# Another order in linear attention, and the first expert sequence's gates and spreading inside its last steps

## What is computed

```python
def linear_attention(x, W_qkv, W_out):
    q, k, v = heads(x @ W_qkv.T)
    q = (elu(q) + 1) * D ** -0.5;  k = elu(k) + 1
    # the result doesn't depend on the size of the chunks
    attn = einsum('bhld,bhmd->bhlm', q, k) * causal
    num = attn @ v + q @ S         # S, Z: sums over the tokens before
    den = attn.sum(-1) + q @ Z
    return (num / maximum(den, 1e-6)) @ W_out.T

def experts(u, centroids, biases, Wr, br, Ws, bs):
    s = softmax(u @ centroids.T + biases)
    g = top-2 of s, zero elsewhere
    routed = einsum('bse,bseo->bso', g, einsum('bsd,eod->bseo', u, Wr) + br)
    return u + routed + (u @ (Ws[0] + Ws[1]).T + bs.sum(0)) / 2
```

## Time and profile before

| | us |
|---|---|
| median of 3 runs (lowest, highest) | 1292.22 (1291.72, 1292.61) |
| the profiled execution | 1292.3 |
| its span | 1290.4 |
| TensorE, VectorE, ScalarE, GpSimd busy | 1151.3, 980.8, 780.4, 563.2 |
| mean granted clock of TensorE | 0.968 |

### The profile page before, as it was taken

One profiled execution on the slowest core, in us unless ns is written; L12 is line 12 of the kernel. 1 busy time (PEld: TensorE's weight loads), 2 busy tenths in 40 slices (PEclk: granted clock), 3 DMA queues, 4 the chain that ended last, 5 costly groups with the idle time before them and its releaser, 6 DMA issues.

```text
span 1290.4 us, 32081 instructions
## 1 busy us (share of the span) xinstructions
PE 1151.3 (89%) x10554; PEld 949.4 (74%) x10554; DVE 980.8 (76%) x2499; ACT 780.4 (60%) x2324; POOL 563.2 (44%) x719
## 2 busy tenths in 40 slices
PE   3888885798989779999999999999999976999997
...
DMA packets 14303, 12.32 MB, mean 10 GB/s; under 512 B 1778, under 2 KB 12564, under 8 KB 13972
## 3 DMA queue, kind: packets, MB, share of 16 engines
...
...
## 4 chain that ended last, share of the span: by engine, by line
PE 45%; DVE 19%; issue 13%; POOL 4%; ACT 2%; DVEq 1%; POOLq 0%; ACTq 0%
PE bank L170 10%; PE bank L955 10%; PE bank L1049 9%; PE bank L1062 5%; PE bank L1020 5%; DVE work L1035 4%; PE bank L819 3%; POOL rstd L344 2%; DVE stat L277 2%; DVE work L1215 2%; DVE work L1207 2%; DVE yn L293 1%; PE bank L774 1%; POOL X L349 1%; DVE fh_hi L1176 1%
## 5 line engine op out<-in xcount | busy, mean ns | idle before, releaser
L972 ACT ACTIVATE work<-bank,work 128x256 f32<-128x256 f32 x512 | 236.0, 473 | 67.1 <-DVE work L964 66.5
L964 DVE TENSOR_REDUCE work<-bank 128x2 f32<-128x512 f32 x256 | 164.2, 684 | 119.6 <-PE bank L955 119.6
L986 POOL TENSOR_TENSOR work<-work 128x512 f32<-128x512 f32 x64 | 66.7, 1042 | 291.3 <-DVE work L980 291.3
L938 POOL TENSOR_TENSOR work<-work 128x512 f32<-128x512 f32 x128 | 164.2, 1283 | 30.8 <-DVE work L930 20.5
L992 ACT ACTIVATE work<-work 128x256 f32<-128x256 f32 x384 | 161.7, 510 | 0.0
L1020 PE MATMUL bank<-ident,work 128*128 128x128 f32 x1024 | 142.2, 281 | 4.9 <-POOL work L986 1.6
L1020 PEld LDWEIGHTS bank<-ident,work 128*128 128x128 f32 x1024 | 113.3, 143 | 36.9 <-issue 24.8
L819 PE MATMUL bank<-WrT,moe_work 128*128 128x128 f32 x1024 | 138.6, 279 | 0.7 <-POOL moe_work L796 0.7
L342 POOL TENSOR_SCALAR ve<-mv 128x2 f32<-128x2 f32 x128 | 28.8, 225 | 243.4 <-DVE mv L282 243.4
L955 PE MATMUL bank<-work 32*128 32x256 f32 x2048 | 131.0, 393 | 3.5 <-DVE work L930 1.7
L1049 PE MATMUL bank<-work 128*64 128x256 f32 x1024 | 127.2, 390 | 6.9 <-DVE work L1035 6.9
...
## 6 DMA issues: line engine op xcount, KB each, us to landing
...
```

Of the source, the lines that this page charges most:

```text
L938: nc.gpsimd.tensor_tensor((QT if kind == "q" else KT)[:, p, a, :], rc[:, ru % 2, :], rs_[:, ru % 2, :], ALU.add).then_inc(c_rope, 1)
L964: nc.vector.tensor_reduce(nmax[:, QUAD * a + j, :], SB_[j][:, :].rearrange("p (t k) -> p t k", t=T), AX.X, ALU.max, negate=True).then_inc( ...
L972: ins = nc.scalar.activation(pr[:, a % 2, j, t, :], SB_[j][:, t * LEN:(t + 1) * LEN], ACT.Exp, bias=nmax[:, h, t:t + 1], accum_out=psum_[: ...
```

## The change

The steps of the linear attention are reordered on three engines. On TensorE the v product comes right behind scores(i, 0), ahead of sums and of the transposition of xn, the output product behind that transposition; ktok, qk and the state product come between sums(i, 0) and their transposition back. v no longer waits for the copied xn; the transposition of o does. On VectorE neg is first in the step and feat is ahead of the statistics of y. On ScalarE the exp is first, the blocks come ahead of the second mask copy, ktok's copy ahead of the sums'. GpSimd makes xT of expert sequences 0 and 1 in steps 14 and 15, TensorE's router for sequence 0 runs inside step 15, and its gates, low half and first three spreadings and scaled products are placed among the remaining attention work. The normalisation of sequence 15 moves into expert steps 0 and 1, three of the ternary check's parts move to expert steps or ahead of them, the two Wsh operations move into attention steps 2 and 3, and the spreading uses its four banks in another order.

The diff, cut (left out: context, and on each engine hunks that only follow from those shown):

Shared functions and GpSimd:

```diff
     pool.wait_ge(last_use, reached(per_seq * (i - 1)))
-    if l == MOE and i_is(i, 0, 1):
-        pool.wait_ge(a_v, SEQS)
+    if l == MOE:
+        if i_is(i, 0, 1):
+            pool.wait_ge(a_v, SEQS - 1 + i)
         pool.wait_ge(n_xnT[1], i + 1)
...
     pe.wait_ge(a_state, reached(i - 1))
-    pe.wait_ge(n_xnT[1], reached(i - 3))
     for t in range(T):
...
 XPAIRS = EXPERTS // 2
-RB, XB, YB_M = bank[1], bank[2:6], bank[6:8]
+RB, XB, YB_M = bank[1], (bank[4], bank[5], bank[3], bank[2]), bank[6:8]
 DVE_PAIRS, FAR = 3 * XPAIRS // 4, 3
...
             pool.wait_ge(z_xnT, CHUNKS)
-        if not i_is(i, SEQS - 2, SEQS - 1):
+        if i_is(i, SEQS - 2, SEQS - 1):
+            pool_xT(pool, MOE, i - (SEQS - 2), p)
+        else:
             pool_xT(pool, LA, i + 2, p)
...
             norm_pool(pool, 1, i - LA_LAG, 1)
+        if not i_is(i, 0, 1, SEQS - 1):
             ffn_excess_pool(pool, i - LA_LAG, p)
...
-    pool_xT(pool, MOE, 0, 0)
-    pool_xT(pool, MOE, 1, 1)
-    for i in range(SEQS - LA_LAG, SEQS):
-        for k in range(ROUNDS[1]):
-            norm_pool(pool, 1, i, k)
-    for i in range(SEQS - LA_LAG, SEQS):
-        ffn_excess_pool(pool, i, i % 2)
-    pool.wait_ge(n_xnT[1], SEQS)
+    rstd_pool(pool, 1, SEQS - 2, 0)
+    residual_pool(pool, 1, SEQS - 2)
+    rstd_pool(pool, 1, SEQS - 2, 1)
+    ffn_excess_pool(pool, SEQS - 3, 1)
...
         if not i_is(i, SEQS - 1):
             moe_far_pool(pool, i + 1, FAR)
+        if i_is(i, 0, 1):
+            ffn_excess_pool(pool, SEQS - 2 + i, p)
```

VectorE:

```diff
         more, live = not i_is(i, SEQS - 1, SEQS), not i_is(i, SEQS)
+        if more:
+            la_feat_vector(dve, i + 1, 1 - p, 0)
         if not i_is(i, 0):
...
                 la_mask_vector(dve, i, 0, g)
+        if more:
+            la_feat_vector(dve, i + 1, 1 - p, 1)
         if not i_is(i, 0, 1):
             run_piece(1, n1, 0, i - LA_LAG, p)
-        if more:
-            la_feat_vector(dve, i + 1, 1 - p, 0)
         if not i_is(i, 0):
...
             run_piece(1, n1, 1, i - LA_LAG, p)
-        if more:
-            la_feat_vector(dve, i + 1, 1 - p, 1)
         if live:
...
         moe_router_vector(dve, rch, 0, 0, part)
-    la_step(SEQS, 0)
-    run_piece(1, n1, 3, SEQS - 2, 0)
+    la_state_vector(dve, SEQS - 1)
+    la_divide_vector(dve, SEQS - 1, 0)
+    run_piece(1, n1, 3, SEQS - 3, 1)
     for part in range(MOE_EXP_PART, MOE_ROUTER_PARTS):
...
     rch.end()
-    for k in range(len(n1)):
-        run_piece(1, n1, k, SEQS - 1, 1)
+    run_piece(1, n1, 0, SEQS - 2, 0)
+    la_divide_vector(dve, SEQS - 1, 1)
+    run_piece(1, n1, 1, SEQS - 2, 0)
     moe_low_vector(dve, 0, 0)
-    for k in range(FAR):
-        moe_scaled_vector(dve, 0, k)
+    moe_scaled_vector(dve, 0, 0)
+    moe_scaled_vector(dve, 0, 1)
+    run_piece(1, n1, 2, SEQS - 2, 0)
+    moe_scaled_vector(dve, 0, 2)
+    run_piece(1, n1, 3, SEQS - 2, 0)
     rch.begin(1)
...
+MOE_LAST_NORM = (1, 2, 5, 7)
 MOE_ORDER = (("norm", 0), ("norm", 1), ("pair", 4), ("late", 4), ("late", 5), ("late", 6), ("late", 7), ("pair", 5),
...
         for what, part in MOE_ORDER:
-            if what == "norm" and not i_is(i, 0):
-                run_piece(2, n2, part, i - 1, 1 - p)
+            if what == "norm":
+                if not i_is(i, 0):
+                    if i_is(i, 1) and part == len(n2) - 1:
+                        dve.wait_ge(n_tp[1], SEQS)
+                    run_piece(2, n2, part, i - 1, 1 - p)
+                elif part in MOE_LAST_NORM:
+                    run_piece(1, n1, MOE_LAST_NORM.index(part), SEQS - 1, 1)
             if what == "early" and not i_is(i, SEQS - 2, SEQS - 1):
```

ScalarE:

```diff
         more, live = not i_is(i, SEQS - 1, SEQS), not i_is(i, SEQS)
+        if more:
+            la_exp_scalar(act, i + 1)
         if live:
             la_mask_scalar(act, i, 0)
+        if more:
+            la_v_scalar(act, i + 1, 1 - p)
         if not i_is(i, 0):
...
         if more:
-            la_v_scalar(act, i + 1, 1 - p)
-            la_exp_scalar(act, i + 1)
+            la_blocks_scalar(act, i + 1, 1 - p)
         if live:
...
             la_turn_scalar(act, i - 1)
-        if more:
-            la_blocks_scalar(act, i + 1, 1 - p)
         if live:
-            la_sums_scalar(act, i, 0)
             la_ktok_scalar(act, i)
+            la_sums_scalar(act, i, 0)
         if not i_is(i, 0, 1, 2):
...
     moe_router_scalar(act, 0, 0)
-    la_step(SEQS, 0)
-    norm_scalar(act, 1, SEQS - 2, TB[:, 0:LEN])
+    la_sums_scalar(act, SEQS - 1, 1)
+    norm_scalar(act, 1, SEQS - 3, TB[:, 0:LEN])
     moe_gates_scalar(act, 0, 0)
-    norm_scalar(act, 1, SEQS - 1, TB[:, 0:LEN])
+    la_turn_scalar(act, SEQS - 1)
+    norm_scalar(act, 1, SEQS - 2, TB[:, 0:LEN])
     act.wait_ge(s_w[SA], 16 * 4)
```

TensorE:

```diff
             la_scores_tensor(pe, i, p, 0)
-        if not i_is(i, 0, 1):
-            la_out_tensor(pe, i - 2)
+        if more:
+            la_v_tensor(pe, i + 1, 1 - p)
         if not i_is(i, 0):
...
         if not i_is(i, 0, 1, 2):
+            pe.wait_ge(a_va, at_most_all(i + 2))
             pe.wait_ge(a_state, i)
             norm_tensor(pe, 1, i - LA_TURN_LAG, TB)
-        if more:
-            la_v_tensor(pe, i + 1, 1 - p)
+        if not i_is(i, 0, 1):
+            la_out_tensor(pe, i - 2)
         if not i_is(i, 0):
...
             la_scores_tensor(pe, i, p, 1)
-        if i_is(i, SEQS - 1, SEQS):
-            pe.wait_ge(n_xnT[1], i - LA_TURN_LAG + 1)
+        if i_is(i, SEQS - 1):
+            pe.wait_ge(s_w[MOE], 16 * 4)
+            pe.wait_ge(a_feat, SEQS)
+            moe_router_tensor(pe, 0, 0)
         if not i_is(i, 0):
+            pe.wait_ge(n_xnT[1], reached(i - LA_TURN_LAG + 1))
             la_turn_tensor(pe, i - 1)
...
             la_sums_tensor(pe, i, p, 0)
+            la_ktok_tensor(pe, i, p)
         if not i_is(i, SEQS - 2, SEQS - 1, SEQS):
...
         if live:
-            la_ktok_tensor(pe, i, p)
-            la_back_tensor(pe, i, 0)
             la_state_tensor(pe, i, p)
+            la_back_tensor(pe, i, 0)
     over_sequences(pe, la_step, 4)
...
-    pe.wait_ge(s_w[MOE], 16 * 4)
-    pe.wait_ge(a_feat, SEQS)
-    moe_router_tensor(pe, 0, 0)
-    la_step(SEQS, 0)
-    la_out_tensor(pe, SEQS - 1)
-    norm_tensor(pe, 1, SEQS - 2, TB)
+    la_sums_tensor(pe, SEQS - 1, 1, 1)
+    pe.wait_ge(a_state, SEQS)
+    norm_tensor(pe, 1, SEQS - 3, TB)
+    la_out_tensor(pe, SEQS - 2)
+    la_back_tensor(pe, SEQS - 1, 1)
     moe_gates_tensor(pe, 0, 0)
-    norm_tensor(pe, 1, SEQS - 1, TB)
-    pe.wait_ge(n_xnT[1], SEQS)
-    pe.wait_ge(a_m, (G4 - 1) * T * SEQS)
-    pe.wait_ge(a_me, T * SEQS)
-    pe.wait_ge(a_o, T * SEQS)
-    pe.wait_ge(n_yn[1], SEQS)
+    pe.wait_ge(n_xnT[1], SEQS - 2)
+    la_turn_tensor(pe, SEQS - 1)
     pe.wait_ge(s_wsh, 2)
...
     pe.wait_ge(s_brlo, 1)
-    for k in range(4):
+    for k in range(FAR):
         moe_spread_tensor(pe, 0, 0, k)
+    la_out_tensor(pe, SEQS - 1)
+    norm_tensor(pe, 1, SEQS - 2, TB)
+    pe.wait_ge(n_xnT[1], SEQS - 1)
+    moe_spread_tensor(pe, 0, 0, FAR)
     moe_router_tensor(pe, 1, 1)
...
                 moe_spread_tensor(pe, i + 1, 1 - p, k - 4)
+            if k == 0 and i_is(i, 1):
+                norm_tensor(pe, 1, SEQS - 1)
             if k == 0 and not i_is(i, 0, 1):
+                if i_is(i, 2):
+                    pe.wait_ge(n_xnT[1], SEQS)
                 norm_tensor(pe, 2, i - 2)
```

39 lines of the change are left out of this document (21 added, 18 removed).

## The result

| | us |
|---|---|
| median of 4 runs (lowest, highest) | 1281.88 (1278.90, 1283.82) |
| beside it the kernel before, 4 runs | 1291.97 |
| ratio, 95% interval | 0.9923 (0.9908 to 0.9938) |
| the profiled execution, its span | 1278.9, 1277.1 |

The change saves 10.1 us. I had forecast 24.6, and 1281.88 lies 3.9 us above the end of my range. The stretches of the profile after show which half came. Busy time of each engine by stretch; the columns are those of the earlier trace rows.

What follows compares the result with a forecast made beforehand. TensorE comes nearest to bounding steady attention steps; between the stages no engine is half busy. Terms -12.8 - 1.7 - 12.4 + 1.0 + 1.3 = -24.6 us gave 1267.5 us, range 1257 to 1278.

Steps and rivals of the forecast that it cites:

- The attention steps, -12.8: Linear attention steps 4 to 14: each falls from 11.07 to 9.91 us, saving 12.8 us (8.9 to 15.7).
- What is late next is VectorE: Steady attention step: VectorE's 9.31 us of busy time plus a 0.60 us wait for rstd give 9.91 us.
- my upper bound of 10.26: Steady attention step: VectorE's present occupation with its short gaps, 9.66 us, plus the rstd wait, at most 10.26 us.
- rival C: Attention steps don't shorten: VectorE, waiting for out, back and rstd, stays near 11 us; 1281 us, chance 0.07.
- My lower bound: Steady attention step: no shorter than the 9.64 us that TensorE alone needs.
- Rival B: Attention steps: VectorE and GpSimd obstruct each other, every xn slow, step 10.22 us; 1271 us (up to 1276), chance 0.18.
- Steps 0 to 3, -1.7: First attention steps, held by GpSimd: TensorE's 1.29 us wait in step 2 goes; 1.7 us saved (0 to 2.7).
- The stretch between the stages, -12.4: From scores(15, 0) to the first expert product: 28.8 us instead of 41.2, sums at the slow clock; 12.4 us saved.
- rival A: Between the stages the clock stays at its full level: -28.9 us in all, 1263.4 us, at best 1257; chance 0.14.
- Rival D: Between the stages no overlap: gates held, spreading still after sequence 15's rows, only steps shorten; 1279 us, chance 0.05.
- Given back, +2.3: First expert steps: +1.0 us for slow clock and sequence 15's normalisation, +1.3 for rstd behind GpSimd's check products.
- Rival E: Attention steps: GpSimd's rstd late behind mask and check products, making the kernel slower, 1302 us with 3 us lateness; chance 0.03.

Runs made afterwards that it cites:

- out_mid: Changed kernel with TensorE's output product moved between the second sums and the transposition of the norm; 1275.30 us, ratio 0.9870.
- after_again: The changed kernel unaltered, run and profiled a second time, against the kernel before; 1282.78 us, ratio 0.9924.

## Why the prediction was right and wrong

- **The attention steps, -12.8: wrong.** The step that failed is "What is late next is VectorE", with its 9.31 + 0.60 = 9.91 us, and it failed twice. First, it took VectorE's order for free of waits for TensorE. The diff put the output product behind the transposition of xn, whose new wait is for the copy of v, that one's for the second sums, and theirs for VectorE's state and division. I counted the copies that the new order covers, and not the two new waits (`a_va` at the transposition, and `a_state` at a v product that now comes early in the step) with the two buffers behind them. The step measured 10.86 us, and 10.31 with both arms of the loop taken out on VectorE, so the loop is 6 of the missing 10.5 us. Second, 9.91 lets VectorE's short gaps between instructions go with the waits. They stayed: in two steps of out_mid (20.69 us) VectorE is busy for 18.64 us, has named waits of 1.38, and 0.67 are left, 0.34 a step against 0.37 in the kernel before. The loop boundary, 0.2 us a step on average, wasn't in the sum at all. So VectorE alone takes 10.3 us in this order, near my upper bound of 10.26, which is the other 4.4 us. That "by my count TensorE and VectorE are within 0.3 us of each other", which I gave as what speaks for rival C, was the place to follow up: the nearer two engines are, the more a wait between them counts.
- **The parts of that step held singly.** The waits for L546 and L371 went; the wait for rstd was 0.54 us of 0.60; and once the output product was moved and a mask put into that wait, the step came to 10.05, written out 9.85 and finally 9.69 us. My lower bound, TensorE's 9.64 us, was reached only by these further edits.
- **Rival C (1281 us, a chance of 0.07) is what happened**, in time and nearly in kind: VectorE, with waits for others in one order, stays near 11 us. The waits are for the output product and rstd; the third that I named, for the transposition back, is gone. I gave it too little because 1.43 us of TensorE's named waits went. They did, and 1.3 us of others came (9.2 in seven steps).
- **Rival B did not come.** It asked for a slow xn in every step. In the change xn took 0.75 and 1.24 us in turn, before 0.62 and 1.19, so VectorE's mean busy time rose from 9.31 to 9.37 us and not to 9.62, and without contention the changed kernel's step is the same. The xn of 0.62 us is no sign against exclusion, as I had read it: its first instruction came when only 0.2 us of the product were left and ended 0.08 us behind it (153.87 against 153.79), and its second ran in the gap between two products but for its last 0.19 us.
- **Steps 0 to 3, -1.7:** -1.6 in the second profile, -2.8 in the first. Step 2, where I had seen the gain, went from 12.82 to 11.20 us in both. Step 3 rose from 12.10 to 12.5 and step 0 moves by itself, so that the sum agrees so well is in part luck.
- **The stretch between the stages, -12.4:** -11.3. The slow level of the clock, on which rival A differed, came: 0.58 in the sums of sequence 15 and 0.84 over the stretch. Rival D fell with it: the first spreading (212.45) stands ahead of the rows of sequence 14.
- **Given back, +2.3:** 2.8 and 4.0 in the two profiles. The check products cost 3.4 to 5.1 us (I took 1.3, with a bound of 3), because the late rstd came in step 1, on the path of TensorE, and its wait of 2.14 us was followed by the slow level of the clock, which that term didn't have. Nothing is left for sequence 15's normalisation (I took 1.0).
- **Rival E:** mask and rstd were never late by GpSimd's own work in the steady steps; GpSimd waited for VectorE's aggregates there, 13.1 us in seven steps.
- The sum of the first profile is -13.6, the medians say -10.1. In after_again the first scores came 1.3 us later, step 0 took 1.2 us more and the stretch to step 2's gates 1.2 more, 3.7 us together: the first profile was of a lucky execution, the shortest of its four.
